# Two mixture tiles mixed by ScalarE and TensorE, logits read from their bank, and the beside-jobs of a fused attention and expert kernel placed anew

## The chip, the cores and the metric

One core of one Trainium2 chip runs the kernel. The metric is the device time of one launch in microseconds (us). Engines are named PE (TensorE), DVE (VectorE), ACT (ScalarE), POOL (GpSimd) and SP (SyncE, which only issues transfers here).

## The reference, cut to what matters

```python
# x (4, 1024, 128); 8 heads of 16; 8 experts, hidden 512, top 2; all float32
def attn(x):                       # on layernorm(x)
    Q, K, V = silu(x @ Wq), silu(x @ Wk), silu(x @ Wv)   # per head
    s = (Q @ K.T + rel_bias[i - j + 255]) / 4            # causal, index clipped
    return (silu(s masked) @ V) * silu(x @ Wu)
def ffn(x):                        # on layernorm(x)
    top_logits, top_idx = top_k(x @ w_gate.T, 2)
    gates = one_hot(top_idx) weighted by softmax(top_logits)
    return sum over e of gates[:, e] * ((x @ w_in[e].T) @ w_out[e].T)
x = x + attn(layernorm(x));  x = x + ffn(layernorm(x))
```

## The kernel before

Each batch has 1024 positions: 8 tiles of 128, in two halves of four. Attention runs as 73 *groups* (`STEPS`, line 60). A group is up to 512 columns of queries against one or two blocks of 128 keys, for four heads, each head in a bank of PSUM of its own (five score banks rotate). Groups belong to *units* of query tiles (`UNITS`, line 37): two halves for each of batches 0 to 2, then for batch 3 tiles 0 to 3 (unit 6), tiles 4 and 5 (unit 7), tiles 6 and 7 (unit 8). For each group PE makes scores (L628, in `scores`), DVE adds the relative bias in the bank (L943, only groups near the diagonal; a third of them need none or half), ACT applies silu (L806, L808) and writes weights to `wts`, PE multiplies them with V into `o_acc` (L644). When a unit is through, DVE multiplies `o_acc` with the gate branch into `oT` (L958).

All other work is written out by hand as *jobs* beside the groups: the list `BESIDE` has one list of jobs for each group, `BEFORE` and `AFTER` hold what comes ahead and behind. Every engine walks the same timeline (L772, L896, L1115, L594) and does its part of each job in order. PE's order in the slot of group g is: scores of group g+1 for heads 0 and 2, the V product of group g-1, the jobs that use a bank, scores of g+1 for heads 1 and 3. DVE: bias of g+1 for heads 0 and 2, the bankless jobs of the slot before, gating, bank jobs, bias for heads 1 and 3. ACT: silu of g for heads 0 and 2, the jobs of the slot before, silu for heads 1 and 3. POOL does its parts one after another.

Jobs: `stats1`/`norm1`/`T1` and `stats2`/`T2` are the layer norms and transposes (statistics on DVE, the power on POOL L508 to L514); `Q`, `K`, `V`, `U` the projections; `MASK` the key mask, which POOL multiplies into the padded V; `split` and SP's transfers build the stacked Q and K of batches 1 to 3; `REL` a bias table on POOL (L588); `WT`, `M`, `CM` fold each expert's two matrices into one, `mm_e`; `SEL` brings the attention result back to rows and DVE adds it (L1016). `LOG` makes the logits on PE, DVE copies them out of the bank (L1022); `best` picks the top two on DVE (L1084 to L1100), `tanh` and `gates` make the two gates (L866, L1106 to L1110). `FF` b, t, part is half of a tile's expert product: 512 columns (four experts) on PE, scaled by the gates on DVE into `ymix` (L1047, one of two buffers, reused once POOL is done with the tile two before); POOL then adds the eight experts in three steps and adds to the tile (L570, L572).

Bank jobs other than the last four use two banks (`jobp`) in turn, so each waits until the job before last has left its bank. The last four, the FF halves of tiles 6 and 7 of batch 3, have the score banks, and DVE mixes them in `mix_last` (L1061): 16 multiply-and-add steps, the two tiles in turn, since each step of a tile needs the one before it. Then SP stores tile 6 and ACT tile 7.

## Time and profile before

| | us |
|---|---|
| median of 3 runs | 286.43 |
| lowest and highest | 283.73, 287.03 |
| the profiled execution, its own time | 283.42 |
| its span (first to last instruction) | 281.5 |

The span leaves out 1.9 us that the launch has around it. In the profile a line number is that of kernel.py; L653 is a helper (`quarters`) that splits one product into four matmuls of 32 output rows, which run side by side, and a float32 matmul shows as two records. So one FF half is 8 records, and a product of 128 columns with four inner steps is 32. A duration in a single row is from start to acknowledged end; the pitch of a run of them (the row's total by its count) is what each costs when they follow each other.

### The profile page before, as it was taken

The page shows a single profiled execution, that of the slowest core. Times are in us where ns is not written, and L with a number is a line of the kernel's source. Part 1 is how long each engine was busy: PE and PEld are TensorE (multiplying, and loading weights), DVE is VectorE, ACT ScalarE, POOL GpSimd, SP SyncE. Part 2 cuts the span into 40 slices and gives each one's busy share as a digit, 9 for nine tenths or more (in the row PEclk, how much of TensorE's full clock was granted, in tenths as well). Part 3 has the DMA queues.
Part 4 walks back from the last instruction along what each step waited for, and adds up shares of the span by engine and source line. Part 5 has one row for each costly group of instructions (what it writes and reads, how often), then busy time and mean ns, then how long its engine had stood idle before and what let it go on. Part 6 is the DMA issues. An engine that isn't in the chain of part 4 may idle for free.

```text
span 281.5 us, 8503 instructions
## 1 busy us (share of the span) xinstructions
PE 264.1 (94%) x3176; PEld 125.9 (45%) x3176; DVE 233.2 (83%) x778; ACT 215.9 (77%) x407; POOL 143.8 (51%) x222
## 2 busy tenths in 40 slices
PE   7599799999998999999999999999999899999991
PEld 5344454555654534343334444333444345554440
DVE  6368544773589998898999979979999989999977
ACT  2677999969876999579989899797767649878600
POOL 6453230331001979485983253569494187286754
PEclk9999999999999999999999999999999999999998
DMA  4797216985931015960169400498890010010011
GB/s 116 168 307 201 77 33 200 222 209 198 224 83 41 1 18 168 238 143 2 43 196 225 104 0 7 155 218 207 231 236 5 2 38 2 2 37 2 10 31 37
DMA packets 27911, 31.23 MB, mean 111 GB/s; under 512 B 3032, under 2 KB 16856, under 8 KB 27872
## 3 DMA queue, kind: packets, MB, share of 16 engines
q1 hardware_dynamic: 24320, 28.28, 39.7%
q10 hardware_dynamic: 3552, 2.43, 3.3%
q8 instruction: 25, 0.41, 0.6%
q14 instruction: 14, 0.11, 0.1%
HBM read 20.73 MB, written 9.98 MB: 109 GB/s over the span
## 4 chain that ended last, share of the span: by engine, by line
PE 53%; DVE 29%; ACT 8%; issue 5%; POOL 3%; DMA 1%; SPq 0%; DVEq 0%; ACTq 0%; POOLq 0%
PE jobp L653 20%; DVE score L943 18%; PE score L628 15%; PE o_acc L644 15%; DVE ymix L1047 4%; ACT wts L808 3%; PE jobp L686 2%; ACT xn L820 2%; ACT wts L806 1%; DVE xs L1061 1%; DVE stats L982 1%; PE jobp L742 1%; PE jobp L722 1%; DMA xs<-in_L_attn_x 1%; POOL ymix L570 1%
## 5 line engine op out<-in xcount | busy, mean ns | idle before, releaser
L806 ACT ACTIVATE wts<-score 128x512 f32<-128x512 f32 (+1 forms) x172 | 98.1, 590 | 32.5 <-DVE score L943 28.5
L943 DVE TENSOR_TENSOR score<-score,bias_near 128x256 f32<-128x256 f32 (+3 forms) x288 | 112.8, 467 | 10.0 <-PE score L628 9.8
L570 POOL TENSOR_TENSOR ymix<-ymix 128x512 f32<-128x512 f32 (+2 forms) x90 | 74.3, 826 | 40.6 <-DVE ymix L1047 35.6
L808 ACT ACTIVATE wts<-score,far 128x512 f32<-128x512 f32 x120 | 74.0, 705 | 7.4 <-DVE score L943 6.8
L644 PE MATMUL o_acc<-wts,v_pad 128*32 128x512 f32 (+3 forms) x864 | 77.1, 458 | 1.3 <-issue 1.0
L653 PE MATMUL jobp<-mm_e,xn2T 128*32 128x512 f32 x480 | 60.0, 593 | 1.3 <-ACT uT L860 1.1
L628 PE MATMUL score<-q_stack,k_stack 64*128 64x256 f32 (+3 forms) x336 | 50.4, 355 | 0.9 <-ACT wts L806 0.4
L628 PEld LDWEIGHTS score<-q_stack,k_stack 64*128 64x128 f32 x336 | 31.1, 184 | 33.2 <-issue 28.3
L1047 DVE TENSOR_TENSOR ymix<-jobp,gates 128x512 f32<-128x512 f32 x60 | 40.5, 685 | 6.2 <-PE jobp L653 5.4
L644 PEld LDWEIGHTS o_acc<-wts,v_pad 128*32 128x32 f32 x864 | 20.8, 108 | 30.3 <-issue 15.3
L558 POOL TENSOR_TENSOR v_pad<-v_s,kmask 128x256 f32<-128x256 f32 x16 | 9.8, 630 | 42.8 <-ACT v_s L853 21.0
L628 PE MATMUL score<-xn2T,xs 32*128 32x512 f32 (+3 forms) x192 | 25.5, 519 | 0.7 <-ACT wts L806 0.7
L653 PEld LDWEIGHTS jobp<-mm_e,xn2T 128*32 128x32 f32 x480 | 15.0, 110 | 24.6 <-issue 17.6
L943 DVE TENSOR_TENSOR score<-score,bias_rel 128x128 f32<-128x128 f32 (+1 forms) x48 | 14.5, 358 | 8.8 <-PE score L628 8.8
L546 POOL TENSOR_TENSOR k_lo<-k,k_hi 128x512 fp32r<-128x512 f32 x6 | 8.2, 1359 | 18.4 <-DVE k_hi L1041 18.4
L508 POOL TENSOR_TENSOR rstd<-mv,eps_t 128x4 f32<-128x4 f32 (+1 forms) x17 | 3.4, 200 | 27.6 <-DVE mv L985 27.5
L628 PEld LDWEIGHTS score<-xn2T,xs 32*128 32x128 f32 x192 | 13.5, 183 | 7.7 <-issue 5.1
L572 POOL TENSOR_TENSOR xs<-xs,ymix 128x128 f32<-128x128 f32 x30 | 13.7, 458 | 2.4
L982 DVE BATCH_NORM_STATS2 stats<-xs 128x6 f32<-128x128 f32 x64 | 14.0, 277 | 0.3 <-DMA xs<-in_L_attn_x 0.2
L820 ACT ACTIVATE xn<-xs,shift,rstd 128x128 f32<-128x128 f32 x28 | 11.5, 486 | 1.7 <-POOL shift L514 1.7
L510 POOL TENSOR_TENSOR rstd<-rstd,mhalf 128x4 f32<-128x4 f32 (+1 forms) x10 | 9.5, 953 | 0.8
L653 PE MATMUL jobp<-xn1T,wq_s 128*32 128x512 f32 x64 | 8.4, 593 | 0.8 <-ACT xn1T L830 0.8
(104 smaller groups left out, 257.4 us busy)
## 6 DMA issues: line engine op xcount, KB each, us to landing
k_stack<-rows_dram SPq DMA_DIRECT2D x24, 256.0 KB, 5.2
q_stack<-rows_dram SPq DMA_DIRECT2D x24, 256.0 KB, 6.8
rows_dram<-k_hi SPq DMA_DIRECT2D x12, 256.0 KB
xs<-in_L_attn_x SPq DMA_DIRECT2D x7, 256.0 KB, 7.8
out<-xs SPq DMA_DIRECT2D x7, 256.0 KB, 6.0
bias_near<-bias_dram SPq DMA_DIRECT2D x4, 384.0 KB, 7.1
rows_dram<-k_lo SPq DMA_DIRECT2D x6, 256.0 KB
rows_dram<-q_hi SPq DMA_DIRECT2D x6, 256.0 KB
```

What stands on the lines that cost most here:

```text
L558: pool.tensor_tensor(v_pad[:, b % 2, ts, 4 * quad:4 * quad + 4, HD * quad:HD * quad + HD], v_s[:, ts].rearrange("p t (j q d) -> p t j q d" ...
L570: then_wait(pool.tensor_tensor(y[:, 0:n], y[:, 0:n], y[:, n:2 * n], ALU.add))
L572: pool.tensor_tensor(xs[:, b, t], xs[:, b, t], y[:, 0], ALU.add).then_inc(tile_done, 1)
L628: ins = pe.matmul(score[bank][:, c:c + n], keys, queries, start=True, stop=True)
L644: ins = pe.matmul(o_acc[32 * j:32 * j + 32, q0:q0 + n], v_pad[:, b % 2, kb, 4 * quad + j, :], wts[:, group % WTS, j, c:c + n], start=USES[ ...
L653: ins = pe.matmul(out[rows], lhsT[:, rows], rhs, start=start, stop=stop)
L806: act.activation(weights, score[bank][:, 0:n], ACT.Silu, scale=HD ** -0.5).then_inc(weighed[bank], 1)
L808: act.activation(weights, score[bank][:, 0:n], ACT.Silu, bias=far[:, h:h + 1], scale=HD ** -0.5)\
L820: ins = act.activation(xn1[:, t], xs[:, b, t], ACT.Identity, bias=shift[:, t:t + 1], scale=rstd[:, 0, t:t + 1])
L943: ins = dve.tensor_tensor(score[bank][:, c + near:c + n], score[bank][:, c + near:c + n], bias, ALU.add)
L982: ins = dve.bn_stats(stats[:, ln, t, :], xs[:, b, t, :])
L1047: drained_by(dve.tensor_tensor(y[:, es], bank_of(job)[:].rearrange("p (e d) -> p e d", d=D), gates[:, t, es].unsqueeze(2).to_broadcast([P, ...
```

## The change

`SUMMED` names products that DVE does not mix any more: all eight experts of tile 5 and experts 4 to 7 of tile 7 (both of batch 3). ACT multiplies each 128x128 piece of the bank by its gate (`product`, an Identity with a scale) into a free `wts` buffer; PE adds them up by matmuls with the identity (`sum_products`), into the fifth score bank and `o_acc`; DVE adds the sum to the tile (`SUM`). POOL no longer adds tile 5. `mix_last` skips experts 4 to 7 of tile 7, so tile 6's last four steps stand alone. Tiles 4, 5 and 6 of batch 3 are stored one by one.

`LOG` no longer copies: the first half of `take_best` follows at once in the same place, reads the logits in their bank and frees it with its second comparison. `best` is now the second half alone.

The lists of jobs are rearranged throughout. Counting slots from 0: slot 2 had `CM2 U00 norm M1 U01 T1 norm` with `M0` ahead and has now `M0 WT2 M1 norm REL`; the old slot 25 (six bank jobs) has shrunk to two, and there are new long ones, slot 20 (seven bank jobs, four of them FF) and slot 28 (nine, five of them FF). `FF 1,7` moves from slot 49 to slots 46 and 48. `U 3,0` moves from slot 39 to 51, `V 3,0` from 43 to 53, `MASK 3,0` from 48 to 52. `FF 3,5,0` moves from behind the last group into slot 72, ahead of the last V product. The order of LOG and FF 3,5,1 after it is turned round.

```diff
+SUMMED = {NT - 3: range(E), NT - 1: range(E // 2, E)}
+SUM_TILES = list(SUMMED)
...
-    [("stats1", 0, 0), ("RB",), ("T1", 0, 0), ("norm1", 0, 0), ("norm1", 0, 1), ("stats1", 0, 1), ("Q", 0, 0),
-     ("K", 0, 0), ("T1", 0, 1), ("V", 0, 0), ("K", 0, 1), ("Q", 0, 1), ("MASK", 0, 0), ("REL",)],
+    [("stats1", 0, 0), ("RB",), ("norm1", 0, 0), ("stats1", 0, 1), ("T1", 0, 0), ("norm1", 0, 1), ("Q", 0, 0),
+     ("K", 0, 0), ("T1", 0, 1), ("V", 0, 0), ("K", 0, 1), ("Q", 0, 1), ("MASK", 0, 0)],
...
-    [("CM", 2), ("U", 0, 0), ("norm1", 1, 0), ("M", 1), ("U", 0, 1), ("T1", 1, 0), ("norm1", 1, 1)],
...
-    [("V", 2, 0), ("U", 1, 1), ("T2", 2), ("T1", 2, 1), ("FF", 0, 4, 0), ("tanh", 1), ("FF", 0, 4, 1)],
...
-    [("FF", 1, 7, 0), ("FF", 1, 7, 1)],
...
-    [("FF", 2, 0, 0), ("MASK", 3, 1)],
...
-    [("FF", 2, 1, 0), ("V", 3, 1)],
...
-    [("best", 5, 0), ("tanh", 5), ("LOG", 5), ("U", 3, 1), ("best", 5, 1), ("gates", 5)],
...
+    [("M", 0), ("WT", 2), ("M", 1), ("norm1", 1, 0), ("REL",)],
...
+    [("FF", 0, 0, 0), ("FF", 0, 0, 1), ("norm1", 2, 0), ("SEL", 1), ("FF", 0, 1, 0), ("FF", 0, 1, 1), ("U", 1, 1),
+     ("T1", 2, 0)],
...
+    [("FF", 0, 4, 0), ("FF", 0, 4, 1), ("T1", 2, 1), ("FF", 0, 5, 0), ("FF", 0, 5, 1), ("FF", 0, 6, 0),
+     ("K", 2, 1), ("LOG", 2), ("best", 2, 1), ("Q", 2, 1), ("tanh", 2), ("gates", 2)],
...
+    [("FF", 1, 6, 1), ("FF", 1, 7, 0), ("LOG", 4), ("best", 4, 1)],
+    [("gates", 4), ("tanh", 4), ("Q", 3, 1)],
+    [("split", 3, 1), ("FF", 1, 7, 1)],
+    [("U", 3, 0)],
+    [("MASK", 3, 0), ("FF", 2, 1, 0)],
+    [("FF", 2, 1, 1), ("V", 3, 0)],
...
+    [("U", 3, 1), ("FF", 2, 3, 0), ("LOG", 5), ("best", 5, 1), ("tanh", 5), ("gates", 5)],
...
+    [("FF", 3, 4, 0)],
+    [("FF", 3, 4, 1), ("FF", 3, 5, 0)],
 ]
 AFTER = [
-    [],
-    [("FF", 3, 5, 0)],
     [],
     [],
     [],
     [],
-    [("T2", 8), ("SEL", 8), ("stats2", 8), ("LOG", 8), ("best", 8, 0), ("best", 8, 1), ("gates", 8),
-     ("FF", 3, 5, 1), ("FF", 3, 6, 0), ("MIX",), ("FF", 3, 7, 0)],
+    [("T2", 8), ("SEL", 8)],
+    [("FF", 3, 5, 1), ("stats2", 8), ("LOG", 8), ("tanh", 8)],
     [],
-    [("tanh", 8), ("FF", 3, 6, 1), ("FF", 3, 7, 1)],
+    [("FF", 3, 6, 0), ("FF", 3, 7, 0), ("best", 8, 1), ("gates", 8), ("SUM", 5), ("MIX",), ("FF", 3, 6, 1),
+     ("FF", 3, 7, 1), ("SUM", 7)],
+    [],
     [],
 ]
...
-        lg = sb("lg", [P, 3, NT, E])
+        lg = sb("lg", [P, 2, NT, E])
...
+        prod = wts[:, (len(ORDER) - 2) % WTS].rearrange("p j (c d) -> p (j c) d", d=D)
+        sums = [score[SCORE_BANKS - 1], o_acc]
...
-            for u in range(2 * B - 4, LAST):
+            for u in range(2 * B - 4, LAST - 1):
                 store(u)
-            sp.wait_ge(last_done[0], 1)
-            sp.dma_start(out[B - 1, (NT - 2) * P:(NT - 1) * P], xs[:, B - 1, NT - 2]).then_inc(stored, 16)
-            sp.wait_ge(stored, 16 * (LAST + len(LAST_TILES)))
+            for t in range(NT - 4, NT - 1):
+                if t in last_done:
+                    sp.wait_ge(last_done[t], 1)
+                else:
+                    sp.wait_ge(tile_done, NT * (B - 1) + t + 1)
+                sp.dma_start(out[B - 1, t * P:(t + 1) * P], xs[:, B - 1, t]).then_inc(stored, 16)
+            sp.wait_ge(stored, 16 * (LAST - 1 + 4))
...
+            def sum_products(t):
+                i = SUM_TILES.index(t)
+                for j in HEADS:
+                    wait_weighed(pe, ORDER[-1], j)
+                pe.wait_ge(gated, LAST + 1)
+                for k, e in enumerate(SUMMED[t]):
+                    if t in LAST_TILES:
+                        pe.wait_ge(scaled_products, k + 1)
+                    elif 2 * e % E == 0:
+                        wait_drained(pe, ("FF", B - 1, t, 2 * e // E))
+                    ins = quarters(sums[i][:, 0:D], ident[:], prod[:, i * E + e],
+                                   start=k == 0, stop=k == len(SUMMED[t]) - 1)
+                ins.then_inc(summed, 1)
...
+            def product(t, e):
+                c = e % (E // 2) * D
+                ins = act.activation(prod[:, SUM_TILES.index(t) * E + e], bank_of(("FF", B - 1, t, 2 * e // E))[:, c:c + D],
+                                     ACT.Identity, scale=gates[:, t, e:e + 1])
...
+                elif kind == "FF" and job[1] == B - 1 and job[2] in SUM_TILES and job[2] not in LAST_TILES:
+                    wait_filled(act, job)
+                    act.wait_ge(gates_ready, LAST)
+                    act.wait_ge(pv_done, len(ORDER) - 1)
+                    half = range(job[3] * E // 2, (job[3] + 1) * E // 2)
+                    for e in half:
+                        ins = product(job[2], e)
+                    drained_by(ins, job)
+                elif kind == "MIX":
+                    wait_filled(act, ("FF", B - 1, NT - 1, 1))
+                    act.wait_ge(gates_ready, LAST + 1)
+                    for e in SUMMED[NT - 1]:
+                        product(NT - 1, e).then_inc(scaled_products, 1)
...
-                    b, tiles = rows_of(args, 1)
-                    wait_filled(dve, job)
-                    ts = slice(tiles[0], tiles[-1] + 1)
-                    drained_by(dve.tensor_copy(lg[:, 0, ts].rearrange("p t e -> p (t e)"), bank_of(job)[:, 0:E * len(tiles)]), job)
+                    take_best(args[0], 0)
                 elif kind == "best":
-                    take_best(*args)
+                    take_best(args[0], 1)
                 elif kind == "gates":
                     mix_gates(*args)
-                elif kind == "FF" and args[:2] not in [(B - 1, t) for t in LAST_TILES]:
+                elif kind == "FF" and args[:2] not in [(B - 1, t) for t in last_done]:
                     b, t, part = args
                     if NT * b + t >= 2:
                         dve.wait_ge(tile_done, NT * b + t - 1)
                     scale_experts(job, ymix[:, t % 2])
                 elif kind == "MIX":
                     mix_last()
+                elif kind == "SUM":
+                    i = SUM_TILES.index(args[0])
+                    dve.wait_ge(summed, i + 1)
+                    dve.tensor_tensor(xs[:, B - 1, args[0]], xs[:, B - 1, args[0]], sums[i][:, 0:D], ALU.add)\
+                        .then_inc(last_done[args[0]], 1)
 
...
+                        if e in SUMMED.get(t, ()):
+                            continue
...
-                    wait_drained(dve, ("LOG", u))
+                    job = ("LOG", u)
+                    logits = bank_of(job)[:, 0:E * n].rearrange("p (t e) -> p t e", e=E)
+                    wait_filled(dve, job)
                     if u == 0:
                         dve.wait_ge(rank_set, E)
-                    for t in tiles:
-                        ins = dve.max(top[:, 0, t], lg[:, 0, t])
+                    for k, t in enumerate(tiles):
+                        ins = dve.max(top[:, 0, t], logits[:, k])
                     then_wait(ins)
-                    for t in tiles:
-                        dve.scalar_tensor_tensor(lg[:, 1, t], lg[:, 0, t], top[:, 0, t, 1:2], rank[:], ALU.is_ge, ALU.mult)
+                    for k, t in enumerate(tiles):
+                        dve.scalar_tensor_tensor(lg[:, 0, t], logits[:, k], top[:, 0, t, 1:2], rank[:], ALU.is_ge, ALU.mult)
                     ins = dve.tensor_tensor(gap[:, ts], top[:, 0, ts, 0], top[:, 0, ts, 1], ALU.subtract)
                     dve.wait_ge(scaled, SCALES.index(((u,), 1)) + 1)
                     then_wait(ins)
                     dve.tensor_tensor(gap[:, ts], gap[:, ts], rstd[:, 1, ts], ALU.mult).then_inc(top_ready, 1)
-                    then_wait(dve.tensor_tensor(lg[:, 2, ts], lg[:, 0, ts], wide(top[:, 0, ts, 1]), ALU.is_gt))
-                    dve.tensor_tensor(pick[:, 1, ts], lg[:, 0, ts], wide(top[:, 0, ts, 0]), ALU.is_equal)
-                    then_wait(dve.scalar_tensor_tensor(lg[:, 1, ts], lg[:, 2, ts], 2.0 * E, lg[:, 1, ts], ALU.mult, ALU.add))
+                    then_wait(dve.tensor_tensor(lg[:, 1, ts], logits, wide(top[:, 0, ts, 1]), ALU.is_gt))
+                    drained_by(dve.tensor_tensor(pick[:, 1, ts], logits, wide(top[:, 0, ts, 0]), ALU.is_equal), job)
+                    then_wait(dve.scalar_tensor_tensor(lg[:, 0, ts], lg[:, 1, ts], 2.0 * E, lg[:, 0, ts], ALU.mult, ALU.add))
                 else:
                     for t in tiles:
-                        ins = dve.max(top[:, 1, t], lg[:, 1, t])
+                        ins = dve.max(top[:, 1, t], lg[:, 0, t])
                     then_wait(ins)
-                    then_wait(dve.tensor_tensor(pick[:, 0, ts], lg[:, 1, ts], wide(top[:, 1, ts, 1]), ALU.is_ge))
+                    then_wait(dve.tensor_tensor(pick[:, 0, ts], lg[:, 0, ts], wide(top[:, 1, ts, 1]), ALU.is_ge))
```

## Rows read from the trace of the kernel before

**Rows 1.** The profile page: the span and the busy time of all engines

```profile
span 281.5 us, 8503 instructions
...
PE 264.1 (94%) x3176; PEld 125.9 (45%) x3176; DVE 233.2 (83%) x778; ACT 215.9 (77%) x407; POOL 143.8 (51%) x222
```

**Rows 2.** The chain of waits: start us, us on the chain, engine, tile, line

```profile
16.27 1.06 PE score L628 x5
...
69.95 0.88 PE jobp L653 x32
...
184.63 1.00 PE o_acc L644 x16
185.63 1.72 PE jobp L653 x16
187.35 0.66 PE score L628 x3
...
209.29 1.27 DVE ymix L1047 x2
...
218.00 2.64 DVE score L943 x8
```

**Rows 3.** Busy time by stretch: A:B, its us, busy us of each engine, PEclk

```profile
22.34:190.54 168.20, 164.61 (x2059) 76.91 (x2059) 136.84 (x457) 147.63 (x282) 76.13 (x109) 1.00 0.50 125
190.54:267.70 77.16, 74.85 (x884) 35.57 (x886) 73.62 (x241) 55.59 (x102) 48.52 (x70) 1.00 0.27 70
267.70:281.50 13.80, 7.72 (x94) 3.25 (x90) 10.13 (x42) 0.57 (x2) 6.72 (x10) 0.90 0.10 29
```

**Rows 4.** Timeline of PE: V products that open slots 2, 3, 56 and 59

```profile
25.89 1.07 PE L644 MATMUL o_acc<-wts,v_pad 128*32 128x384 f32 x16
...
33.27 1.07 PE L644 MATMUL o_acc<-wts,v_pad 128*32 128x512 f32 x8
...
213.61 1.07 PE L644 MATMUL o_acc<-wts,v_pad 128*32 128x384 f32 x16
...
226.10 1.07 PE L644 MATMUL o_acc<-wts,v_pad 128*32 128x256 f32 x16
```

**Rows 5.** Single lines of DVE: ns min/median/max, first and last start, forms

```profile
L1022 DVE COPY lg<-jobp x9: 142/178/193, 59.3 to 271.9; 128x32 f32<-128x32 f32 x7, 128x16 f32<-128x16 f32 x2
...
L1010 DVE TENSOR_SCALAR kmask<-jobp x8: 178/181/193, 16.8 to 196.6; 128x32 f32<-128x32 f32 x8
...
L1093 DVE TENSOR_TENSOR lg<-lg,top x9: 164/182/184, 63.1 to 273.2; 128x32 f32<-128x32 f32 x7, 128x16 f32<-128x16 f32 x2
```

**Rows 6.** Single lines of ACT and DVE, same columns as the group above

```profile
L883 ACT COPY mm_e<-jobp x8: 258/262/393, 24.8 to 78.5; 128x128 f32<-128x128 f32 x8
...
L820 ACT ACTIVATE xn<-xs,shift,rstd x28: 477/484/504, 10.3 to 147.7; 128x128 f32<-128x128 f32 x28
...
L1061 DVE SCALAR_TENSOR_TENSOR xs<-score,gates,xs x16: 340/340/341, 275.3 to 279.1; 128x128 f32<-128x128 f32 x16
```

**Rows 7.** Timeline of the tail: start us, us, engine, line, operation, idle before

```profile
267.70 0.86 PE L644 MATMUL o_acc<-wts,v_pad 128*32 128x256 f32 x16
...
268.35 1.07 PE L653 MATMUL jobp<-mm_e,xn2T 128*32 128x512 f32 x8
...
269.35 0.71 PE L684 MATMUL jobp<-ident,xs 128*128 128x128 f32 x4
...
272.13 3.62 PE L653 MATMUL score<-mm_e,xn2T 128*32 128x512 f32 x32
...
274.65 0.69 DVE L1047 TENSOR_TENSOR ymix<-jobp,gates 128x512 f32<-128x512 f32 x1
...
275.26 4.22 DVE L1061 SCALAR_TENSOR_TENSOR xs<-score,gates,xs 128x128 f32<-128x128 f32 x16
275.49 2.60 POOL L570 TENSOR_TENSOR ymix<-ymix 128x512 f32<-128x512 f32 x3 [2.43 <-DVE ymix L1047]
```

## What I expect, and how it is worked out

> **What bounds the kernel now.** I read the page first [rows 1]: PE is busy 264.1 of the 281.5 us span, DVE 233.2, and both run at full clock. Neither share says which of the two sets the time, since a PE that waits inside a chain of matmuls still counts as busy. So I read the chain of waits next [rows 2]. Up to about 190 us it is made almost wholly of PE pieces that follow each other without a gap: one group of attention costs 0.66 us of scores and 1.00 us of weights times V, and each FF half, Q, K or U beside it 0.86 us (1.72 for two). From 190 to 222 us the chain runs through DVE: eight bias additions of a group in 2.64 us, two FF scalings in 1.27 us (0.64 each). The busy times by stretch [rows 3] say the same: DVE is busy 136.8 of 168.2 us (81%) before 190.54, and 73.6 of 77.2 us (95%) from there to the last group. In the last 13.8 us no engine is full; a chain of dependent steps sets the end.
>
> I call "slot g" the jobs listed beside group g. Pricing every slot's PE work with the rows' figures (first batch's scores 1.07 instead of 0.66 [rows 2]; V or M 0.88; transposes about 0.5, logits 0.25), slots 1 to 48 hold 157.5 us of PE work and take 168.2; slots 49 to 72 hold 69.0 of PE and take 77.2. Some 19 us of the body are thus not PE work. They sit in a few slots [rows 4]: slot 2 takes 7.38 us (25.89 to 33.27) for 6.0 of PE work, and slots 56 to 58 take 12.49 us (213.61 to 226.10) for 8.3.
>
> **The change, part by part.**
>
> *The logits' copy goes.* Nine copies [rows 5], seven of 0.18 us and two of 0.15: 1.5 us of DVE. Three of them (0.5 us) lie in the stretch that DVE binds, one (0.14) in the tail, the rest under PE cover and worth nothing. The operations that now read the logits' bank: the mask reads a bank in 0.181 us and the comparison of the same 128x32 reads SBUF in 0.182 [rows 5], so I charge nothing; the upper bound is the spread of those two rows, 0.193 less 0.164, 0.03 us an operation. By the Trainium skill ("Perfetto Trace Analysis", Optimizing Scalar/DVE Operations), DVE's access overhead is about 60 ns on SBUF and about 125 on PSUM; by that figure the 82 operations would cost 5.3 us more of DVE, an estimate. The rows above do not show that difference. The bank is also held longer: the copy freed it 0.18 us after DVE reached it, now the second comparison does, about 1.5 to 2 us later. The job after next needs this bank; between lie one other job (0.86) and the next group's scores and V product (1.66), 2.5 us in nearly every slot. Cost nothing; bound 0.5 us each where DVE lags, four times, 2 us.
>
> *Tile 5 leaves DVE and POOL.* Its two scalings (0.64 each) go to ACT, which is busy 0.57 us in the last 13.8 [rows 3]. Eight products: each at least 0.262 us (copy of a 128x128 bank piece) and at most 0.484 (scaled Identity, 128x128) [rows 6]; cover from idle ACT is complete. One of them lay between the last V product and the transposes (slot AFTER, below). PE gains 8 x 4 quarter matmuls of 128 columns: an M job has 16 of these in 0.88 us [rows 2], so SUM 5 costs 1.76 and SUM 7 0.88.
>
> *Placement.* Between the lists, what crosses the border of slot 48/49 counts. FF 1,7's two halves move forward out of the DVE stretch (DVE -1.28, PE -1.72); U(3,0), V(3,0), MASK(3,0) move into it (PE +2.0, DVE +0.18), and FF(3,5,0) enters slot 72 on ACT (PE +0.86). So slots 49 to 72: DVE -1.28 -0.5 +0.18 = **-1.6 us**, PE +1.15 (to 70.2, still under the 77). Since DVE binds here I take the whole -1.6; bound from below -0.5, as PE draws level in slots 61 to 72 (34.2 of PE against 33.7 of DVE by my sums), from above -4, if the stall of slots 56 to 58 (4.2 us, DVE busy with gates while PE waits for U's drain) shrinks with it. Slots 0 to 48: PE +1.72 -2.0 = **-0.3 us**; DVE +0.4 where it has room. REL (3.7 us of POOL) moves two slots down, far before slot 7 that needs it; SP's loads and the splits stay at least six slots ahead of their readers. Bounds of this part: -3 (slot 2 loses two PE jobs and an ACT job, and its 1.4 us stall with them) to +3 (crowded slots, below).
>
> *Tail* [rows 7]. Now: the last V product ends at 268.56 and an FF half stands between it and the transposes at 269.35; in the new order that half is already done, so all that follows starts about 0.75 earlier. Logits and FF(3,5,1) then end at 271.4, FF(3,6,0) and (3,7,0) at 273.1, SUM 5 at 274.9, the last two halves at 276.6 and their results at 276.8. DVE has the gates by about 274.2 (now 274.65, less what POOL, still adding tile 4, lets through of the 0.75) but must wait for SUM 5: its addition (0.27) ends at 275.3, just where the 16-step mix starts now (275.26). The mix: eight interleaved steps at 4.22/16 = 0.264 make 2.1 us (277.4); the last four of tile 6 stand alone, each waits for the one before, so at least the operation's own 0.340 [rows 6], say 0.36: 1.45 us (278.85). Beside it ACT makes four products from 276.8 (1.0 to 1.9 us), PE adds each (0.22): 278.2 to 279.0, hidden. The last addition ends at 279.1; now the mix ends at 279.48. **-0.4 us**, bounds -1.2 and +0.5. POOL's additions for tile 5 were not on this path.
>
> **Sum.** -1.6 -0.3 -0.4 = -2.3 us: span 281.5 becomes 279.2, the profiled run (283.42) 281.1. That run is at the fast end of the runs shown (median 286.43, lowest 283.73), so against the median I forecast 286.43 - 2.3 = **284.1 us**.
>
> **Rivals.**
> 1. *The placement also recovers stalls.* For it: 19 us of the body are no PE work, and 5.6 of them stand in the slots of [rows 4], of which slot 2 is thinned and 56 to 58 differ. Against: slots 55 to 60 hold 25.5 us of DVE work, as before (25.7 by my sums). With slot 2's stall gone, half of that of 56 to 58 and 1.5 elsewhere: 1.4 + 2.1 + 1.5 = 5.0 more, 279.1 us.
> 2. *Slower: the crowded slots.* Slot 28 now has nine bank jobs beside one group, 8.4 us of PE work, and slot 20 seven with 7.0. ACT and DVE have half a group's scores to work on meanwhile. Slot 2 now loses 1.4 us on 6.0 (23%) [rows 4]; at that rate these two lose 3.5 us. The five FF halves of slot 28 also meet POOL, which needs 2.60 us [rows 7] and one more addition (some 3.1 us) a tile before a buffer is free again: DVE's FF(0,6,0) comes about 0.7 us too early. Over 2.3 us lost beyond today's, it decides: 284.1 + 3.5 + 0.7 = 288.3 us. Against: in such a slot PE is fed by jobs alone, two banks alternate, and an FF half leaves its bank in 0.64 us [rows 2], under PE's 0.86.
> 3. *Reads from the bank are dearer.* 28 operations from slot 49 on at 0.03 us each: +0.8, 284.9 us. By the skill's figure named above it would be 28 x 65 ns = 1.8 us, 285.9, an estimate.
> 4. *The change doesn't reach the end.* DVE's 1.6 us is handed to PE, and SUM 5 before the mix eats the tail: 286 us.
>
> **Chances.** Forecast 0.42 (its own range 282.5 to 285.5), stalls recovered 0.21, crowded slots 0.20, dearer reads 0.07, no reach 0.10. The range takes the others in: 280.0 to 288.3. Two per cent is 5.7 us, and about what a measurement here can tell from no change; faster than 280.7 holds most of rival 1 and nothing else: 0.17. Slower than 292.2 needs more than rival 2 gives: 0.08. Within: 0.75.
>
> **What would show it.** In the profile after: the stretch from slot 49's V product to slot 72's should be near 75.6 us, with DVE still above 93% busy; the stretch before it near 168, without new gaps around slots 20 and 28 (two pitches of 7 to 8.5 us). Transposes should start right behind the last V product; DVE should idle some 0.8 us between gates and SUM 5's addition; tile 6's last four steps should come at 0.35 us each. The MAX8 and the scoring operations should last what they do now. I am wrong if the crowded slots last over 10 us, if PE waits for the logits' bank, or if the stretch of slots 49 to 72 turns out bound by PE.

## The result, and the profile after

| | median of the runs | profiled execution | its span | granted clock, mean |
|---|---|---|---|---|
| before | 284.69 us (283.03 to 287.03, 20 runs) | 283.42 | 281.5 | 0.995 |
| after | 287.77 us (286.03 to 289.86, 20 runs) | 289.01 | 287.3 | 0.988 |

The changed kernel takes 1.0099 times as long, interval 1.0076 to 1.0123: 2.8 us more (2.2 to 3.5; the medians differ by 3.1), where I had forecast 2.3 us less. The three runs of before that the forecast was tied to (median 286.43) lay high; against the 20 it would have read 282.4. Executions that ran at a clearly lower clock and over 1.5% longer than the fastest of their kernel (one each of e1 and e9, five of e10) are left out of the medians and ratios.

Three stretches of the kernel after, cut at the same V products as [rows 3]; columns as there:

```profile
22.60:198.13 175.53, 170.77 (x2015) 77.05 (x2011) 137.25 (x457) 146.75 (x279) 81.98 (x116) 0.98 0.49 120
198.13:273.89 75.76, 73.31 (x931) 35.05 (x931) 73.39 (x236) 56.69 (x105) 46.39 (x64) 1.00 0.27 67
273.89:287.30 13.41, 9.81 (x182) 5.47 (x178) 7.62 (x36) 4.01 (x14) 3.83 (x6) 1.00 0.11 31
```

Beside [rows 3]: slots 49 to 72 took 75.76 us for 77.16 (-1.40, forecast -1.6), the tail 13.41 for 13.80 (-0.39, forecast -0.4). The whole loss stands in the first stretch: 175.53 for 168.20, +7.33 us, forecast -0.3. The profiled executions lie at opposite ends of their runs, so they differ by 5.6 us where the medians differ by 3.1. A part of this is the clock: 0.995 and 0.988 in these two, while the mean over all executions is 0.994 for after and 0.990 to 0.991 for the executions of before that were timed beside the experiments. So the clock does not make after the slower one in the medians.

That stretch loses first in slot 1. Timeline of PE there (start us, us, engine, line, operation, idle before it and its releaser):

```profile
25.97 0.29 PE L668 MATMUL jobp<-wg_s,centre 128*32 128x8 f32 x8 [2.30 <-DMA wg_s<-in_L_ffn_w_gate]
26.19 1.12 PE L757 MATMUL jobp<-ident,wout_s 128*128 128x128 f32 x4
27.24 2.10 PE L643 MATMUL score<-xn2T,xs 32*128 32x512 f32 x12
29.27 1.94 PE L659 MATMUL o_acc<-wts,v_pad 128*32 128x384 f32 x16
```

CM 2, the centring of w_gate, is now the first job of slot 1. Its 4 KB were issued by SP behind the loads of four experts. The issues on SP's queue (0.90 is the issue, not the transfer; the view of transfers gives 5.4 us from issue to landing):

```profile
19.93 0.43 SPq L413 DMA_DIRECT2D ymix<-in_L_ffn_w_in  x1
20.40 0.90 SPq L471 DMA_DIRECT2D wg_s<-in_L_ffn_w_gate  x1
```

20.40 + 5.4 = 25.8, and PE stood still 2.30 us for it. The kernel before had as little to spare, which its trace would have told: issue at 21.45, 5.3 us to landing, 26.75, and its only reader, a slot later, starts 0.2 us behind that:

```profile
21.45 0.90 SPq L460 DMA_DIRECT2D wg_s<-in_L_ffn_w_gate  x1
```
```profile
26.92 0.25 PE L653 MATMUL jobp<-wg_s,centre 128*32 128x8 f32 x8
```

Then, in the profiled execution of after, the clock fell. Busy time by windows of 4 us, columns as in [rows 3]:

```profile
20.00:24.00 4.00, 3.66 (x33) 1.39 (x32) 2.63 (x8) 3.30 (x7) 0.00 (x0) 1.00 1.00 290
24.00:28.00 4.00, 2.03 (x16) 1.47 (x20) 1.30 (x3) 2.62 (x6) 0.00 (x0) 0.71 0.06 8
28.00:32.00 4.00, 4.00 (x48) 2.44 (x44) 2.56 (x7) 1.76 (x3) 0.00 (x0) 0.50 0.03 6
```

PE was busy 2.03 of the 4 us up to 28, and for the next 4 us it was granted 0.50 of its clock, 1.2 GHz, while busy all the time. The kernel before shows 1.00 in the same three windows. Not every execution pays this: e12 below has the same lists there and a wait of 2.43 us, and its windows show 1.00 throughout; its slots 1 to 3 take 15.4 us for the 17.0 here. So of the 4.2 us that slots 1 to 3 lose here more than before, some 1.6 are the clock, and 2.6 come with the wait.

The remaining loss is spread. (Slot g ends at the V product of group g, as in the prediction.) The table prices each slot's PE jobs with the figures of the forecast and gives what the slots took beyond them, from the V products of the traces; the last column is an experiment told below, in which the wait is gone:

| slots | before | after | after, w_gate loaded early |
|---|---|---|---|
| 1 to 3 | 1.6 | 5.8 | 1.9 |
| 4 to 18 | 3.7 | 4.6 | 3.7 |
| 19 to 28 | 2.3 | 4.2 | 4.1 |
| 29 to 35 | 1.1 | 1.1 | 1.1 |
| 36 to 41 | 1.2 | 3.2 | 3.2 |
| 42 to 48 | 0.8 | 0.4 | 0.4 |
| 49 to 59 | 6.5 | 4.1 | 4.1 |
| 60 to 72 | 1.7 | 1.6 | 1.6 |

Slots 20 and 28, the crowded ones, took 8.65 us for 6.96 of PE work and 9.91 for 8.43. The tail, beside [rows 7], from the timeline of after:

```profile
273.89 0.86 PE L659 MATMUL o_acc<-wts,v_pad 128*32 128x256 f32 x16
...
274.68 0.71 PE L699 MATMUL jobp<-ident,xs 128*128 128x128 f32 x4
...
279.18 1.93 PE L668 MATMUL score<-wts,ident 128*32 128x128 f32 x64
...
279.92 0.18 DVE L1169 SCALAR_TENSOR_TENSOR gates<-pick 128x16 f32<-128x16 f32 x1
...
281.25 0.29 DVE L1086 TENSOR_TENSOR xs<-xs,score 128x128 f32<-128x128 f32 x1 [1.15 <-PE score L668]
281.45 3.57 DVE L1117 SCALAR_TENSOR_TENSOR xs<-score,gates,xs 128x128 f32<-128x128 f32 x12
282.90 1.14 ACT L846 ACTIVATE wts<-score,gates 128x128 f32<-128x128 f32 x4 [3.93 <-PE score L668]
283.41 1.11 PE L668 MATMUL o_acc<-wts,ident 128*32 128x128 f32 x32 [0.58 <-ACT wts L846]
284.94 0.28 DVE L1086 TENSOR_TENSOR xs<-xs,o_acc 128x128 f32<-128x128 f32 x1
```

The transposes start 0.79 us behind the last V product's start (1.65 before), DVE idles 1.15 us for SUM 5, and twelve mix steps take 3.57.

### The profile page after: what moved, and what is told of

Its sections match the earlier page's. It is cut to its first block, busy times and chain, and to the rows that moved or that the text cites. A ratio compares the mean times of both kernels' runs of the same rounds, so it can differ in the third digit from the quotient of the medians.

```text
span 287.3 us, 8701 instructions
## 1 busy us (share of the span) xinstructions
PE 270.8 (94%) x3272; PEld 127.4 (44%) x3272; DVE 230.2 (80%) x765; ACT 219.8 (77%) x419; POOL 141.0 (49%) x218
## 3 DMA queue, kind: packets, MB, share of 16 engines
q10 hardware_dynamic: 3552, 2.43, 3.0%
## 4 chain that ended last, share of the span: by engine, by line
PE 52%; DVE 35%; SPq 4%; issue 3%; DMA 2%; POOL 1%; ACT 1%; DVEq 0%; POOLq 0%
DVE score L995 20%; PE jobp L668 18%; PE o_acc L659 14%; PE score L643 13%; DVE ymix L1101 7%; DMA wg_s<-in_L_ffn_w_gate 2%; DVE stats L1034 2%; SPq L412 2%; PE jobp L701 2%; PE jobp L757 1%; PE score L668 1%; DVE xs L1117 1%; PE jobp L737 1%; SPq L462 1%; SPq L413 1%
## 5 line engine op out<-in xcount | busy, mean ns | idle before, releaser
L585 POOL TENSOR_TENSOR ymix<-ymix 128x512 f32<-128x512 f32 (+2 forms) x87 | 72.2, 830 | 35.6 <-DVE ymix L1101 31.0
L659 PE MATMUL o_acc<-wts,v_pad 128*32 128x512 f32 (+3 forms) x864 | 78.8, 463 | 0.4 <-ACT wts L839 0.4
L643 PE MATMUL score<-q_stack,k_stack 64*128 64x256 f32 (+3 forms) x336 | 48.5, 355 | 0.4 <-ACT wts L839 0.2
L643 PEld LDWEIGHTS score<-q_stack,k_stack 64*128 64x128 f32 x336 | 30.0, 184 | 33.3 <-issue 29.5
L1101 DVE TENSOR_TENSOR ymix<-jobp,gates 128x512 f32<-128x512 f32 x58 | 39.2, 683 | 6.4 <-PE jobp L668 4.7
L643 PE MATMUL score<-xn2T,xs 32*128 32x512 f32 (+3 forms) x192 | 27.2, 541 | 0.7 <-ACT wts L839 0.7
L668 PEld LDWEIGHTS jobp<-mm_e,xn2T 128*32 128x32 f32 x480 | 14.3, 110 | 22.0 <-issue 13.0
L587 POOL TENSOR_TENSOR xs<-xs,ymix 128x128 f32<-128x128 f32 x29 | 13.3, 459 | 2.3
L1034 DVE BATCH_NORM_STATS2 stats<-xs 128x6 f32<-128x128 f32 x64 | 13.9, 276 | 0.3 <-DMA xs<-in_L_attn_x 0.2
```

Of the source, the lines that this page charges most:

```text
L585: then_wait(pool.tensor_tensor(y[:, 0:n], y[:, 0:n], y[:, n:2 * n], ALU.add))
L587: pool.tensor_tensor(xs[:, b, t], xs[:, b, t], y[:, 0], ALU.add).then_inc(tile_done, 1)
L643: ins = pe.matmul(score[bank][:, c:c + n], keys, queries, start=True, stop=True)
L659: ins = pe.matmul(o_acc[32 * j:32 * j + 32, q0:q0 + n], v_pad[:, b % 2, kb, 4 * quad + j, :], wts[:, group % WTS, j, c:c + n], start=USES[ ...
L668: ins = pe.matmul(out[rows], lhsT[:, rows], rhs, start=start, stop=stop)
L1034: ins = dve.bn_stats(stats[:, ln, t, :], xs[:, b, t, :])
```

## The experiments

The profiled execution of each is cut at the V products of slots 0, 48 and 72. "Ratio" is to the kernel before on the same chip.

| run | median us (runs) | ratio, 95% | slots 1 to 48 | 49 to 72 | tail |
|---|---|---|---|---|---|
| before | 284.69 (20) | | 168.2 | 77.2 | 13.8 |
| after | 287.77 (20) | 1.0099, 1.0076 to 1.0123 | 175.5 | 75.8 | 13.4 |
| e1_cm2_later | 287.58 (9) | 1.0091, 1.0052 to 1.013 | 172.9 | 75.8 | 13.4 |
| e2_cm2_in_before | 289.60 (6) | 1.0149, 1.0101 to 1.0196 | 173.4 | 77.2 | 13.9 |
| e3_tail_alone | 286.60 (12) | 1.0036, 1.0001 to 1.0071 | 168.0 | 78.5 | 13.3 |
| e4_slot28_spread | 290.55 (6) | 1.020, 1.0155 to 1.0246 | 176.8 | 76.0 | 13.4 |
| e5_cm2_slot8 | 286.08 (10) | 1.0041, 1.0005 to 1.0078 | 171.7 | 75.8 | 13.4 |
| e6_even_slots | 292.33 (4) | 1.0241, 1.0192 to 1.0291 | 177.4 | 76.1 | 13.4 |
| e7_copy_back | 290.31 (5) | 1.0189, 1.0133 to 1.0246 | 173.8 | 76.4 | 13.4 |
| e8_hybrid | 288.61 (4) | 1.0113, 1.0058 to 1.0169 | 171.8 | 79.9 | 12.8 |
| e9_join33 | 290.06 (5) | 1.021, 1.0157 to 1.0263 | 176.4 | 75.8 | 12.5 |
| e10_join18 | 286.75 (7) | 1.0052, 1.0008 to 1.0096 | - | - | - |
| e11_gate_load_early | 285.56 (12) | 1.0026, 0.9995 to 1.0056 | 170.7 | 75.8 | 13.3 |
| e12_sum5_late | 287.53 (12) | 1.0079, 1.005 to 1.0108 | 173.5 | 75.8 | 12.5 |
| e13_join33_copied | 283.42 (12) | 0.9962, 0.9934 to 0.999 | 169.6 | 75.8 | 12.6 |
| e14_join38_copied | 283.94 (12) | 0.9986, 0.9949 to 1.0023 | 170.1 | 75.8 | 12.5 |
| e15_gate_load_and_sum5 | 284.13 (12) | 0.9977, 0.994 to 1.0015 | 171.6 | 75.8 | 12.5 |

### The load of w_gate

Theory A: CM 2, moved ahead of its data, makes PE wait in slot 1, and the clock may fall behind the wait. First the move alone, in the kernel before:

```diff
-    [("M", 0), ("WT", 1), ("stats1", 1, 1)],
-    [("CM", 2), ("U", 0, 0), ("norm1", 1, 0), ...
+    [("CM", 2), ("M", 0), ("WT", 1), ("stats1", 1, 1)],
+    [("U", 0, 0), ("norm1", 1, 0), ...
```

> The kernel before with only CM 2 moved one slot forward, to the head of slot 1, as the change has it. Theory A: PE waits 2 to 3 us for the transfer, the clock falls, slots 1 to 3 take 3 to 4 us more, and the kernel is 2.5 to 4 us slower than before (1.010 to 1.014). Theory B: no difference, since nothing else is touched.

1.5% slower than before, 4.2 us. Its timeline of PE and one window:

```profile
26.37 0.30 PE L653 MATMUL jobp<-wg_s,centre 128*32 128x8 f32 x8 [2.86 <-DMA wg_s<-in_L_ffn_w_gate]
```
```profile
28.00:32.00 4.00, 4.00 (x29) 2.13 (x24) 0.39 (x1) 0.85 (x2) 0.00 (x0) 0.50 0.39 131
```

A 2.86 us wait, then half the clock: in this execution every V product behind slot 1 is 5.3 to 5.5 us late, and nothing else differs. Here the clock has a share in the median too: the mean granted clock of the six executions is 0.985, for 0.990 of before. Then the other way round, CM 2 out of the way in the kernel after, to the end of slot 3 and, since that met another wait, to slot 8:

```diff
-    [("CM", 2), ("WT", 1), ("stats1", 1, 0)],
+    [("WT", 1), ("stats1", 1, 0)],
-    [("stats1", 1, 1), ("M", 2), ("T1", 1, 0)],
+    [("stats1", 1, 1), ("M", 2), ("T1", 1, 0), ("CM", 2)],   e1_cm2_later
-    [("K", 1, 1)],
+    [("CM", 2), ("K", 1, 1)],                                e5_cm2_slot8
```

> The changed kernel with one job moved: CM 2, the only reader of the gate weights' transfer, goes from the head of slot 1 to the end of slot 3. Theory A (PE waits 2.3 us for that transfer and then runs at a granted clock of 0.5 to 0.7 until 32 us): slots 1 to 3 lose about 1.6 us over their PE work as in the kernel before, not 5.8; the clock stays at 1.00; the V product of slot 4 comes about 4 us earlier, and the kernel is 2.5 to 4 us faster than the changed one, level with the kernel before. Theory B (crowded slots 20 and 28 are the cause): under 1 us gained, 287 us.

> The changed kernel with CM 2 in slot 8, ahead of K 1,1: neither at the transfer's landing (25.8 us) nor third in a slot, where the end of slot 3 made it wait 1.3 us for the bank that ACT empties. Theory A (transfer wait 2.3 us and its clock): slots 1 to 18 take 64 to 65 us where the changed kernel took 68.6 and the kernel before 68.1, and the kernel is 2 us or more below the changed one's 287.8, 285.5. Theory B (crowded slots and third jobs): 287 us, the gain is under 1.

In slot 3 CM 2 is the third job for two banks, and waits until ACT has emptied M 2's:

```profile
36.80 0.25 PE L668 MATMUL jobp<-wg_s,centre 128*32 128x8 f32 x8 [1.29 <-ACT mm_e L935]
```

so in the median nothing was won (287.6 us, where 2.5 to 4 us less had been expected). This wait alone does not explain that: in the profiled execution slots 1 to 3 took 13.6 us for 17.0, and slots 4 to 48 only 0.8 more than in after; the rest stays open. In slot 8 it gave back 1.7 us. Last the cure at the source: the lists as they are, the load three experts earlier in SP's queue, behind the first expert's.

```diff
             load_expert(0)
             load_x(1, 1)
+            sp.dma_start(wg_s[:], w_gate.rearrange("e d -> d e"), allow_slow_non_contiguous=True).then_inc(wg_in, 16)
             load_expert(1)
             load_expert(2)
             load_expert(3)
-            sp.dma_start(wg_s[:], w_gate.rearrange("e d -> d e"), allow_slow_non_contiguous=True).then_inc(wg_in, 16)
```

> The kernel after, with one line of SP's queue moved: the load of w_gate is issued behind the first expert's load, ahead of the last x half and of two expert loads, not behind them all. CM 2 stays at the head of slot 1. Theory A (the load is what slot 1 waits for, and the fall of the granted clock behind it follows from the wait): it lands before 24, the 2.30 us ahead of CM 2 goes, slots 1 to 3 lose no more than the kernel before's, and the time is 286.1 +- 0.6, that of the run with CM 2 in slot 8. Rival (CM 2 at this place costs by itself, or the later expert loads are then late): 287.5 or more, with another wait in slots 1 to 3.

Its issue on SP's queue and CM 2 in PE's timeline, without a wait:

```profile
14.68 2.09 SPq L468 DMA_DIRECT2D wg_s<-in_L_ffn_w_gate  x1
```
```profile
25.14 0.21 PE L668 MATMUL jobp<-wg_s,centre 128*32 128x8 f32 x8
```

Issued at 14.68, 7.7 us to landing, 22.4: no wait. 285.56 us, 2.2 of the 3.1 us are back, and slots 1 to 3 lose 1.9 us, about what they lose before (table above). CM 2's place costs nothing once its data is there; theory A holds for the wait, and it is the largest single part. For the clock it is not shown in after: with the wait 0.994 in the mean, without it (e11) 0.996.

### The crowded slots

Theory B: the jobs piled into slots 20 and 28 cost more than their PE time. The test spreads them, first slot 28's over slots 28 to 33 (e4), then slots 19 to 39 with at most four bank jobs each, in a kernel with CM 2 in slot 8 (e6). Cores of the edits, the lists of the new slots:

```diff
+    [("FF", 0, 5, 0), ("K", 2, 1), ("LOG", 2)],                              e4, slot 29
+    [("V", 2, 1), ("FF", 1, 0, 0), ("FF", 1, 0, 1), ("U", 2, 1), ...],       e4, slot 33
+    [("FF", 0, 7, 1), ("U", 2, 1), ("MASK", 2, 0)],                          e6, slot 33
```

> The changed kernel with slots 28 to 33 evened out: at most four bank jobs beside a group, where slot 28 had nine; same jobs, same order of the FF halves. Theory B (crowding makes PE wait for banks that DVE and POOL hold): slot 28's loss over its PE work, 1.5 us, goes to 0.3, and the six slots together take 1 to 1.5 us less (they take 25.4 now), the kernel about 1.2 us less. Theory A (the transfer is the whole loss): same time as the changed kernel.

> As the run before it (CM 2 in slot 8), and slots 19 to 39 rearranged so that none has more than four bank jobs, and that a job which ACT empties has at most one bank job behind it in its slot. The rule: ACT empties a slot's banks only after the next group's first two silus, so the second bank job behind such a one waits. Theory B: slots 19 to 39 take 76 us or less (changed kernel 78.2, before 72.7 with 4.6 us less PE work), their loss over PE work falls from 7.5 to 4, and the kernel comes to 282 to 284 us, under the kernel before. Theory A alone: same time as the run before it.

Both got slower, against the expectations. In e4 slots 28 to 32 gained 4.4 us, but 2.6 of that is PE work that went into slot 33; slot 33, with 5.4 us of PE work, took 10.4, and the six slots together 28.4 us for 25.4. In e6 slot 33 took 7.2 us, and slots 19 to 39 took 83.8 for 78.2. Timelines of PE, e4 and then e6:

```profile
147.42 1.11 PE L667 MATMUL jobp<-mm_e,xn2T 128*32 128x512 f32 x8 [2.31 <-ACT v_s L891]
```
```profile
144.80 1.06 PE L666 MATMUL jobp<-mm_e,xn2T 128*32 128x512 f32 x8 [0.92 <-DVE ymix L1099]
...
149.09 0.27 PE L666 MATMUL jobp<-headsum,kabs 128*32 128x8 bf16 x16 [2.36 <-DVE ymix L1099]
```

There are two banks for jobs. The third bank job of a slot starts when DVE or ACT has drained the first, and behind each engine's queue stand the next group's bias additions and the statistics. So what costs here is less how many jobs stand in a slot than which one must drain when its drainer is busy with something else: the three waits above are 2.3, 0.9 and 2.4 us, while the crowded slot 28 as a whole loses 1.5 us on 8.4. Theory B in the form I gave it (a cost per job) falls.

### The tail

```diff
-    [("FF", 3, 6, 0), ("FF", 3, 7, 0), ("best", 8, 1), ("gates", 8), ("SUM", 5), ("MIX",), ("FF", 3, 6, 1),
-     ("FF", 3, 7, 1), ("SUM", 7)],
+    [("FF", 3, 6, 0), ("FF", 3, 7, 0), ("best", 8, 1), ("gates", 8), ("MIX",), ("FF", 3, 6, 1),
+     ("FF", 3, 7, 1), ("SUM", 5), ("SUM", 7)],                               e12_sum5_late
```

e3 gives the kernel before the new tail alone, its lists and copy kept, with FF 3,5,0 a third job of slot 72.

> The kernel before, its lists and its copy of the logits kept, with the tail of the change alone: tile 5 and half of tile 7 mixed by ACT and PE, FF 3,5,0 in slot 72, the new order behind the last group. The tail was sized at -0.4 us, and the traces show 13.80 and 13.41 us behind the last V product's start. Expected: last stretch 13.3 to 13.6 us, but slot 72 has one FF half more of PE work (+0.86): the whole within 0.5 us of the kernel before. If the tail were the loss, it would be slower by 2 us or more.

> The kernel after, with SUM 5 behind the last four FF halves instead of ahead of them. In the tail DVE waits 1.15 us for SUM 5 before it starts the scaling of the last halves; with SUM 5 late it should start them at once and add tile 5 while TensorE sums tile 7. Expected: tail 12.7 in place of 13.4 us, and 0.7 us off the time, 287.1. Rival (ACT's four scaled products and SUM 7 set the end): no change, 287.8.

> The kernel after with both single repairs: w_gate's load issued behind the first expert's, and SUM 5 behind the last four FF halves. Expected 285.56 - 0.25 to 0.9 = 285.0, between 284.4 and 285.5: no slower than the kernel before. If it stays below 284.5, the repairs alone beat the kernel before; if above 285.5 the later SUM 5 brings nothing.

e3: the tail is 0.5 us shorter, but slot 72 takes 3.9 us for 2.6, because the half put there has to fit beside the last group: 1.0036 of before, so the tail alone is no gain. In after that half displaces another. e12: in its timeline DVE starts the mix 0.21 us behind the start of the last gate operation, in after 1.53 us behind it:

```profile
278.20 0.17 DVE L1169 SCALAR_TENSOR_TENSOR gates<-pick 128x16 f32<-128x16 f32 x1
278.41 3.58 DVE L1117 SCALAR_TENSOR_TENSOR xs<-score,gates,xs 128x128 f32<-128x128 f32 x12
...
281.91 0.28 DVE L1086 TENSOR_TENSOR xs<-xs,score 128x128 f32<-128x128 f32 x1
282.10 0.28 DVE L1086 TENSOR_TENSOR xs<-xs,o_acc 128x128 f32<-128x128 f32 x1
```

The tail falls from 13.4 to 12.5 us in this and in every later kernel with that order. The medians show it less surely: 0.2 us between after and e12, 1.4 between e11 and e15. Both repairs together, e15, are level with before (284.13 us, where 285.0 was expected).

### The logits' bank, and lists joined

What is left, 2 to 3 us between the repaired kernel and the forecast, had to be in the lists or in reading the logits from their bank. e7 puts the copy back into the kernel after; e8 joins the kernel before's slots 0 to 48 (with the copy everywhere) to after's 49 to 72 and the later SUM 5; e9 and e10 join them at slots 33 and 18, with the logits read in their bank, as after has it, and the later SUM 5 too. (In e10 the two FF halves that before's slot 17 has already done fall away from slot 20.)

```diff
+                    drained_by(dve.tensor_copy(lg[:, 0, ts]..., bank_of(job)[:, 0:E * len(tiles)]), job)
                     take_best(args[0], 0)      (reads lg, no longer the bank)
```

> The changed kernel with the copy of the logits back: DVE copies them (0.15 to 0.18 us, nine times), frees the bank at once and goes on from SBUF; nothing else differs. If the reads from the bank or the longer hold (1.5 to 2 us) cost what a rival had (0.8 us, or 1.8 by the page's figure), this kernel is that much faster than the changed one. My expectation: the same within 0.5 us, since MAX8 takes 0.156 us from the bank against 0.151 from SBUF; it may be 0.5 us slower by the copies in the stretch that DVE binds.

> The lists of the kernel before for slots 0 to 48 (U 3,0, V 3,0 and MASK 3,0 taken out, the last FF halves of batch 1 one slot earlier), those of the change from slot 49 on and its tail, with the copy of the logits kept, and SUM 5 put behind the last FF halves so that the mix need not wait for it. If my sums hold (first stretch -0.3, second -1.6, tail -0.4, and the mix 0.8 to 1 us earlier): 2.5 to 3.3 us less than the kernel before, about 282 us; first stretch at or under 168.5 us, second 75.5 to 76, last 12.5. If the first stretch's loss came from moving the FF halves forward and not from the wait and the crowded slots, its time would again be several us over 168.

> The kernel after with the kernel before's lists for slots 0 to 33 (with before's start, CM 2 in slot 2 and REL ahead of the loop) and its own from slot 34 on, and SUM 5 put behind the last four FF halves. The logits are read from their bank throughout. Theory A (what the change loses lies in slots 1, 20 and 28, what it gains in slots 49 to 72 and the tail): the V product of group 33 starts where the kernel before has it, slots 34 to 48 cost up to 1.2 us more than before, slots 49 to 72 give 1.4, the tail 0.4 and the later SUM 5 0.7 more: 284.7 - 1.3 = 283.4, between 282.5 and 284.3. Rival B (the stretch of slots 34 to 48 carries the loss): the time stays at 285.5 or more, and the first stretch is 2 us or more over the 168.2 of before.

> As the last one, but the kernel before's lists for slots 0 to 18 alone, and the kernel after's from slot 19 on. Slot 20 loses FF 0,0,0 and FF 0,0,1 (both already done in slot 17), slot 28 keeps its eleven jobs. Theory A: if slot 28 costs 1.5 us of its own, this one lies 1 to 1.5 us above the join at slot 33, near 284.7; if slot 28 only holds what its neighbours had before, the two agree within 0.5. Slot 20 should fall from 8.65 us to below 7.5.

e7: 2.5 us slower than after, where the same within 0.5 us had been expected; its profiled execution is its fastest, and shows 0.7 of it in slots 49 to 72. There the removed copy is worth what the forecast said. Another 0.5 stands in slots 4 to 48 (158.7 us for the 158.2 of e12, whose clock did not fall either); the rest of the 2.5 is not placed. In e7 the first pass over the logits still stands at once behind the copy, so it frees the bank early and leaves DVE's order as it is: no gain from the shorter hold of the bank shows in after's lists.

e8 is the largest miss: 282 us expected, 288.61 measured, 1.1% over before. Its slot 48 takes 4.2 us for the 2.6 of before, slots 64 and 70 take 5.6 and 3.7 for the 3.4 and 2.5 of after, and in its profiled execution the clock stood at 0.50 from 20 to 24 us. It has the first passes over units 6 and 7 a slot behind their LOG, in lists made for the pass in the bank; whether that is the cause was not tested.

e10's profiled execution (412.66 us) ran at 0.56 of the clock throughout and can't be read by slots. Its median, 286.75 us, lies 2 us above its expectation of 284.7; it does not separate slot 20 from slot 28 and stays inconclusive.

e9 was the miss that taught most. It had the lists of before up to slot 33, no stall in slot 1, and was 2.1% slower than before, where 283.4 us had been expected. V products agree with before to 0.8 us up to group 24's; slot 25 then took 11.4 us instead of 6.9 (the expectation of e13 counts it, and the two others it names, one lower). Its PE, DVE and ACT timelines there, three views one after the other:

```profile
112.28 1.06 PE L666 MATMUL jobp<-wv_s,xn1T 128*32 128x128 f32 x32
114.40 1.06 PE L666 MATMUL jobp<-xn1T,wu_s 128*32 128x512 f32 x8 [1.06 <-DVE pick L1151]
117.91 1.11 PE L699 MATMUL jobp<-ident,xs 128*128 128x128 f32 x4 [2.44 <-ACT v_s L890]
```
```profile
111.06 0.38 DVE L1141 MAX8 top<-jobp 128x8 f32<-128x8 f32 x4
...
112.02 1.20 DVE L1145 TENSOR_TENSOR gap<-top 128x4 f32<-128x4 f32 x1
113.32 0.69 DVE L1149 TENSOR_TENSOR gap<-gap,rstd 128x4 f32<-128x4 f32 x1
...
114.15 0.19 DVE L1151 TENSOR_TENSOR pick<-jobp,top 128x32 f32<-128x32 f32 x1
...
114.61 1.16 DVE L993 TENSOR_TENSOR score<-score,bias_rel 128x128 f32<-128x128 f32 x4
...
120.71 0.19 DVE L1163 SCALAR_TENSOR_TENSOR pick<-pick,half_tanh 128x32 f32<-128x32 f32 x1 [4.44 <-ACT half_tanh L916]
```
```profile
114.95 2.42 ACT L839 ACTIVATE wts<-score,far 128x512 f32<-128x512 f32 x4 [3.46 <-DVE score L993]
117.24 0.61 ACT L890 ACTIVATE v_s<-jobp 128x512 f32<-128x512 f32 x1
```

With the copy gone, the whole first pass over the logits (111.06 to 114.34; in after's own place for it 1.7 us) stands where the 0.18 us copy stood. Half of its 3.3 us is not its own work: L1145 and L1149, which have medians of 0.16 us, lasted 1.20 and 0.69 here, beside three additions of POOL (from 111.92, 2.62 us). In before one operation of the pass is stretched in the same way (L1087, 1.31 us for a median of 0.22, also beside POOL's additions), but there the bias additions are already done. That POOL is the cause no run tests. Two things wait for the end of the pass. The bank: U 1,1, two bank jobs behind LOG 1, waits 1.06 us. And DVE's own queue: four bias additions start 3.2 us behind the V product of group 24 (111.39), where before they started 0.24 ahead of it, so ACT's weights, then ACT's copy of V, then the transposes behind it (2.44 us), then the tanh that the gates need (DVE stands 4.44 us). To tell this from the lists alone, e13 is e9 with the copy kept for units 0 to 2 alone, whose LOG lies in the kernel before's lists:

```diff
+                    if args[0] < 3:
+                        drained_by(dve.tensor_copy(lg[:, 2, ts]..., bank_of(job)[:, 0:E * len(tiles)]), job)
+                    else:
                         take_best(args[0], 0)
```

> The join at slot 33, with one thing changed: the logits of units 0 to 2 (the three whose LOG lies in the kernel before's lists) are copied out of their bank as the kernel before does, those of units 3 to 8 are read in it. Theory H (the bank is held through the whole first pass over the logits, 3.4 us in slot 24, and what the kernel before's lists put behind a LOG waits for it): slot 24 falls from 11.4 back to 6.9 us, slots 9 and 27 from 4.5+0.8 and 4.86 to what the kernel before has, the V product of group 33 starts where the kernel before has it (143.7), and the time is 290.2 - 6.3 = 283.9, between 283.0 and 284.8. Rival (it is the gates that wait for ACT's tanh, whatever holds the bank): slot 24 stays above 10 us and the time above 288.

> As the last one, but the kernel before's lists to slot 38 and the kernel after's from slot 39 on (stats2 3 in slot 39, as the kernel before has it). In the kernel after slots 36 to 41 wait 3.2 us over their TensorE work, in the kernel before 1.2. If that loss lies in the lists of slots 36 to 38, this kernel is 1.0 faster than the join at slot 33: 282.9. If it lies in reading the logits of unit 3 from their bank in slot 40, the two agree within 0.4.

The same place in e13, DVE's timeline and then PE's:

```profile
112.17 0.18 DVE L1073 COPY lg<-jobp 128x32 f32<-128x32 f32 x1
112.27 1.15 DVE L993 TENSOR_TENSOR score<-score,bias_rel 128x128 f32<-128x128 f32 x4
```
```profile
114.27 1.04 PE L666 MATMUL jobp<-xn1T,wu_s 128*32 128x512 f32 x8
115.56 0.66 PE L699 MATMUL jobp<-ident,xs 128*128 128x128 f32 x4 [0.25 <-ACT v_s L890]
```

Slot 25 (112.51 to 119.40) took 6.9 us again, U 1,1 waits for nothing, and the kernel 283.42 us: 6.6 less than e9, forecast 6.3. Of the 6.9 us between the first stretches of the two, 4.6 stand in slot 25, 1.1 in slot 28, 0.9 in slot 32. The copy takes away both the hold and the place ahead of the bias additions; no run with before's lists tells the two apart. e13 is 0.4% faster than before, 0.9934 to 0.999, and by the ratios 3.9 us faster than after: the fastest of the kernels timed. e14 agrees with it within 0.5 us. There slot 36 took 3.05 us for the 4.06 that e13 and after need, but the loss returned in slot 41 (4.54 us for 3.35), behind unit 3's logits read in the bank (timeline of PE; oT stands in DVE's queue behind the first pass and an FF scaling):

```profile
169.59 0.63 PE L735 MATMUL jobp<-ident,oT 128*128 128x128 f32 x4 [1.08 <-DVE oT L1008]
```

So slots 34 to 48 take 48.0 us in e13 and 48.5 in e14, for 46.8 before: 1.2 to 1.6 us that neither arrangement avoids. A kernel that differs from e14 by the copy for unit 3 alone was not run; e8, which has that copy and before's lists, takes 6.4 us for slots 40 and 41, e14 7.4, before 6.2.

## Why the prediction was right or wrong

**Slots 49 to 72: the number right, the step behind it not.** -1.40 for -1.6, and DVE is busy 73.4 of 75.8 us (97%). But the forecast took the whole of it from DVE having 1.6 us less to do, and DVE's busy time fell by 0.23 us only (73.62 to 73.39). The copies are gone, but the scalings cost 17.41 us in the stretch for 18.04, 0.6 less and not 1.28: in before DVE did the last half of tile 4 mostly behind the border, and now does it ahead of it. And DVE's two casts for split 3,1, listed in slot 48 now, came over the border and were not counted. In before they stand at 186.5; in after:

```profile
199.14 0.42 DVE L1095 CAST k_hi<-k 128x512 fp32r<-128x512 f32 x1
199.47 0.42 DVE L1095 CAST q_hi<-q 128x512 fp32r<-128x512 f32 x1
```

Single small operations also lasted longer (one comparison, L1159, 1.28 us for a median of 0.19). What shrank is DVE's idle time, from 3.5 to 2.4 us: it waited 3.3 us for FF halves of PE, in eight places, before, and 1.0 us, in three, after. That the sum came out so near is in good part luck. The stretch comes again at 75.8 us in eight other kernels with those lists, at 76.0 and 76.1 in e4 and e6, 76.4 in e7 and 79.9 in e8. What slots 56 to 58 lose fell from 4.2 to 2.5 us.

**Tail: right in sum and in its steps.** -0.39 for -0.4. The idle before SUM 5's addition was 1.15 us for 0.8, ACT's products had a pitch of 0.285 (bounds 0.262 and 0.484), the twelve mix steps 3.57 us for 2.1 + 1.45. I had seen that SUM 5 holds the mix back and not drawn the conclusion that it should stand behind the last halves: 0.9 us.

**Bank reads: right.** MAX8 and the comparison, from their lines in after (columns as in [rows 5]):

```profile
L1143 DVE MAX8 top<-jobp x32: 154/156/175, 66.7 to 277.8; 128x8 f32<-128x8 f32 x32
```
```profile
L1153 DVE TENSOR_TENSOR pick<-jobp,top x9: 174/191/192, 68.2 to 278.9; 128x32 f32<-128x32 f32 x7, 128x16 f32<-128x16 f32 x2
```

The kernel before's MAX8 on SBUF has a median of 151 ns, and its L1094 the same 192 as the comparison here: at most 5 ns dearer, 0.2 us over 32 MAX8. (The operations that read the bank from slot 49 on are 32, six of them in the tail, and not 28; it changes nothing.) By the Trainium skill ("Perfetto Trace Analysis", Optimizing Scalar/DVE Operations) some 65 ns more were to be expected; the measurement decides against it for these operations.

**The jobs moved to early slots: the failed step.** "SP's loads and the splits stay at least six slots ahead of their readers" was said for all and checked for none of the first three slots. CM 2 moved from slot 2 to the head of slot 1, with its load at the end of SP's queue: 2.3 us of wait. In the forecast it stands at nothing, inside "slots 0 to 48: -0.3 us", and the bound of +3 was drawn for the crowded slots, not for it; the stretch came out at +7.33, beyond that bound. e11 measures it: 2.2 us in the medians. My slot 2 argument (two PE jobs fewer, stall gone) was right by itself: in e11 the slot loses 0.6 us for 1.4.

**The hold of the bank: right for the lists of after, and only for them.** I priced the hold alone, and left out that the first pass also moves ahead of the bias additions in DVE's queue; with before's lists the two cost 6.6 us (e9 against e13), above my bound of 2. Copy and placement must thus be judged together: the copy put back into after's lists costs too (e7).

**Crowded slots: the rival was right that they cost, wrong in what it compared with.** Slots 20 and 28 lose 1.7 and 1.5 us, 3.2 together, near its 3.5. But it added this to what the kernel loses today, and the slots around them lose less than before: slots 19 to 28 lose 4.2 us for 2.3, so +1.8 where I had 3.5 + 0.7. (DVE did wait for a buffer of POOL in slot 28, once, 0.5 us for the 0.7.) Not counted at all were slots 36 to 41, +2.0, which no rival named; e14 shows the loss moving from slot 36 to slot 41, and its cause stays open.

**The sum, made again** from the profiled executions and the table of slots: w_gate's wait 2.6 and the clock 1.6, slots 4 to 18 +0.9, 19 to 28 +1.8, 36 to 41 +2.0, 42 to 48 -0.4; the PE work of slots 1 to 48 falls by 1.1 (the 0.3 of the forecast, and U 0,0, which moved ahead of them). Together +7.4 for the measured +7.33. With -1.40 and -0.39 the span grows by 5.5, and the first V product starts 0.25 later: 5.8. In the medians 2.2 of the 3.1 us is the load; the other 0.9 is what is left of the lists' losses after the gains in slots 49 to 72 and in the tail.

## What to carry to other kernels

Before a reader of a load moves forward by even one slot, add up the issue time of its load and its landing: here the slack was 0.2 us, and the slot that was given away 3.5. Moving the load ahead in its queue was the cheaper cure: it cost nothing that the runs show. When an operation that only copied a bank out is removed, look at what now stands in its place in the queue, and who is behind it: here 0.18 us became 3.3. Jobs that share two banks are limited by the engine that drains the third job's bank, so count what that engine has queued at that moment, not the jobs. And where engines hand work to each other, a busy time that stays the same can hide a gain in the waits, and the other way round: read both.

## What the runs showed of the hardware

Behind waits of nearly the same length TensorE's clock was down in some executions and not in others. Behind 2.30 us (after) and 2.86 us (e2) a whole window of 4 us ran at 0.50, 1.2 GHz, with PE busy all the time; behind 2.18 us (e7) and 2.43 us (e12) it stayed at 1.00; the two windows of e12 stand below, columns as in [rows 3]. By the Trainium skill ("TensorE: Matmul & The Clock Gate", Part 1) 1.2 and 2.4 GHz are the two levels; the windows at 0.50 and 1.00 agree, and those in between are means over 4 us.

```profile
24.00:28.00 4.00, 1.64 (x23) 1.23 (x24) 1.57 (x4) 2.89 (x6) 0.00 (x0) 1.00 0.12 21
28.00:32.00 4.00, 2.89 (x67) 1.95 (x65) 3.58 (x13) 2.58 (x6) 0.00 (x0) 1.00 0.02 6
```

The clock also dips in some executions without such a wait. In e11 the window 20 to 24 us has PE busy 4.00 of 4.00 at 0.65 of the clock, in before the same window has 1.00 (e1, e3, e5 and e8 show 0.50 to 0.59 there):

```profile
20.00:24.00 4.00, 4.00 (x29) 2.01 (x32) 1.39 (x5) 2.85 (x6) 0.00 (x0) 0.65 0.80 204
```

It moved e11's first V product to 23.95 (22.35 before), and comparing single profiled executions by their spans would have charged 1.6 us to the change. Why it comes is not known from these runs.

The 4 KB of w_gate took 5.4 us from issue to landing behind the loads of four experts (after) and 7.7 us when issued earlier, beside other transfers (e11); the 256 KB loads of expert matrices in after took 5.3 to 7.7.
